# A transformer block with a top-2 mixture of experts: half of the router moved into a pause of attention

## The reference, cut to what matters

```
x: (4, 1024, 128) float32, 16 heads of width 8, 8 experts of width 512, top 2
sa, ca, ga, sb, cb, gb = modulation of each of the four batches
h = layernorm(x) * (1 + ca) + sa
q, k, v = h @ Wq + bq, h @ Wk + bk, h @ Wv + bv
scores = q k^T / sqrt(8), kept where |i - j| <= half   (half at most 60)
x = x + ga * (per-head W_o of softmax(scores) v, then @ Wfc + bfc)
h = layernorm(x) * (1 + cb) + sb
score = relu(h @ rw1 + rb1) @ rw2 + rb2                # (4096, 8)
gate = softmax over the two highest scores of a token, 0 elsewhere
out = sum over e of gate[:, e] * (relu(h @ W1[e] + b1[e]) @ W2[e] + b2[e])
x = x + gb * out
```

## Time and profile before

| | |
|---|---|
| median of 3 runs | 541.64 us (540.28 to 542.08) |
| the profiled execution | 538.34 us, span 536.5 us |
| PE busy | 453.1 us, 84% |
| DVE | 378.4 us, 71% |
| ACT | 349.0 us, 65% |
| POOL | 369.7 us, 69% |

### The profile page before, as it was taken

The page is one execution under the profiler, slowest core; times in us unless marked ns, Lnnn a source line. Parts: engine busy times, 40 slices in busy tenths (PEclk is TensorE's granted clock), DMA queues, the critical chain, the costliest instruction groups (busy, mean ns, idle before and its releaser), DMA issues.

```text
span 536.5 us, 16755 instructions
## 1 busy us (share of the span) xinstructions
PE 453.1 (84%) x5323; PEld 356.0 (66%) x5323; DVE 378.4 (71%) x1026; ACT 349.0 (65%) x1521; POOL 369.7 (69%) x586
## 2 busy tenths in 40 slices
PE   6998888888888888887929996659668999999977
PEld 5565666666666666665504446658447999999977
DVE  6777999999999999999493565735332554555654
ACT  3668999999999999999523552424023787756800
POOL 6975655556688668764447879875888877777640
PEclk9999999999999999999876996969557999999979
DMA  9351000000000400301311121222211222224446
GB/s 236 83 172 46 13 12 13 13 12 13 14 13 12 111 14 14 91 12 44 99 44 34 51 83 51 81 70 79 91 60 61 80 71 82 69 81 137 133 135 194
DMA packets 61519, 36.54 MB, mean 68 GB/s; under 512 B 25806, under 2 KB 57334, under 8 KB 61306
## 3 DMA queue, kind: packets, MB, share of 16 engines
q1 hardware_dynamic: 55834, 25.83, 18.4%
q0 software_dynamic: 4352, 9.45, 5.2%
q10 hardware_dynamic: 1248, 0.20, 0.2%
HBM read 20.56 MB, written 14.88 MB: 66 GB/s over the span
## 4 chain that ended last, share of the span: by engine, by line
PE 35%; DVE 22%; ACT 21%; issue 12%; another core or an unknown queue 5%; POOL 2%; DVEq 2%; ACTq 0%; POOLq 0%
ACT pr L1026 20%; PE pAm L1935 9%; DVE nmax L1093 8%; PE pAm L1485 5%; PE pSpm L1943 5%; PE pScm L1943 4%; PE pScm L1255 2%; DVE oT L947 1%; PE pScm L1500 1%; DVE w1t L1793 1%; DVEq L1552 1%; PE pm L767 1%; DVE stat L1337 1%; PE pSpm L1492 1%
## 5 line engine op out<-in xcount | busy, mean ns | idle before, releaser
L1026 ACT ACTIVATE pr<-pS,nmax 128x136 f32<-128x136 f32 x512 | 185.5, 382 | 13.4 <-DVE nmax L1093 13.2
L1700 ACT ACTIVATE act<-pAm,w1t 128x128 f32<-128x128 f32 x288 | 82.6, 377 | 85.4 <-PE pAm L1935 41.2
L1026 ACT ACTIVATION_READ_ACCUMULATOR pr<-pS,nmax 128x1 f32 x512 | 108.8, 212 | 0.0
L1935 PE MATMUL pAm<-hgT,w1t 128*128 128x128 f32 x576 | 87.2, 293 | 19.3 <-issue 12.8
L1055 PE MATMUL pS<-kT,qbd 64*128 64x136 f32 x1024 | 93.8, 302 | 1.5 <-ACT pr L1026 1.2
L1935 PEld LDWEIGHTS pAm<-hgT,w1t 128*128 128x128 f32 x576 | 77.6, 206 | 24.7 <-issue 20.0
L1647 POOL DMA_INDIRECT y_scr<-ys,si x72 | 73.2, 1016 | 29.7 <-DVE ys L1809 18.0
L1093 DVE TENSOR_REDUCE nmax<-pS 128x4 f32<-128x544 f32 x128 | 87.6, 685 | 2.1 <-PE pS L1059 1.4
L1101 DVE STREAM_TRANSPOSE prT<-pr 128x640 f32<-128x640 f32 x96 | 81.1, 845 | 8.9 <-ACT pr L1026 0.2
L1055 PEld LDWEIGHTS pS<-kT,qbd 64*128 64x128 f32 x1024 | 68.3, 186 | 14.6 <-ACT pr L1026 1.1
L1614 POOL DMA_INDIRECT xs<-h_all,pos_i x64 | 64.0, 999 | 11.3 <-issue 9.6
(11 more groups left out here) (304 smaller groups left out, 716.4 us busy)
## 6 DMA issues: line engine op xcount, KB each, us to landing
hg<-xs SPq DMA_DIRECT2D x72, 72.0 KB
vbd<-v_scr SPq DMA_DIRECT2D x132, 16.0 KB, 1.7
v_scr<-h_all SPq DMA_DIRECT2D x8, 256.0 KB, 2.3
h_all<-y_scr SPq DMA_DIRECT2D x8, 256.0 KB, 3.1
w_all<-y_scr SPq DMA_DIRECT2D x8, 256.0 KB, 5.0
x_all<-in_L_attn_x SPq DMA_DIRECT2D x3, 512.0 KB, 6.1
w_all<-in_L_ffn_W SPq DMA_DIRECT2D x2, 768.0 KB, 4.9
w_all<-in_L_ffn_W SPq DMA_DIRECT2D x3, 512.0 KB, 5.1
```

Source lines behind the costliest of these rows:

```text
L1026: e.activation(pr[:, n, to:to + SPAN], scored(j, gi)[:, lo:lo + SPAN], ACT.Exp, bias=nmax[:, k:k + 1], scale=-1.0, accum_out=rs[u][:, k:k ...
L1700: e.activation(ac(u)[:, k, :], pU[u % W][:, k, :], ACT.Relu, bias=w1t[u // 2 % 4][:, u % 2, FF + D + k:FF + D + k + 1]).then_inc(a_up.sem, 1)
L1935: mm = e.matmul(pU[u % W][:, k, :], w1t[u // 2 % 4][:, u % 2, k * P:(k + 1) * P], hgT[u // 2 % 4][:, u % 2, :], start=True, stop=True)
```

## The change

Attention stops in front of step 20 (FIRST = NT // 2 + 4), and all engines run the router of groups 0 to 3 (G1 = 4) there, in `first_half_*`. Parts 0 and 1 get choices and places in the pause. The choices of part 2 follow behind steps 20 and 21 on DVE, its place in step 23. POOL sends 28 of the first half's 32 dispatches in steps 20 to 31, up to three per step (`send`), without a memset behind them, and the other four after attention. Roots now go by groups of four tiles: on POOL for groups 0 to 2, on DVE for group 3 (in front of the pause), 4 and 5 (a third behind each of steps 23 to 25 and 27 to 29), 6 and 7 (after attention). Behind attention there are four groups. DVE makes both lists of the first half between the scores of groups 4 and 5. In the expert stage the place of part 4 comes at turn 5, and POOL sends two scatters (SOON) ahead of part 4.

```
+            NP1 = 3
+            G1 = NG // 2
+            FIRST = NT // 2 + 4
-            RANKED = 9
+            RANKED = 5
+            SOON = 2
-            BEHIND = {0: 6, 5: 8, 6: 10, 7: 12}
+            BEHIND = {0: 6}
...
+                def send(t, k):
+                    if t < FIRST or sent[0] == NT or k and t % 4 >= 2 and t >= FIRST + 6:
+                        return
+                    if sent[0] == 2 * PARTS[NP1 - 1][0]:
+                        routed(e, NP1 - 1)
+                    dispatch(e, sent[0] // 2, sent[0] % 2)
+                    sent[0] += 1
...
                 def step(i, u, j):
                     maxima(i, u, j, 0)
+                    if 2 * i + u == FIRST:
+                        token_scores(e, G1 - 1)
+                    if 2 * i + u == FIRST + 3:
+                        place(e, NP1 - 1)
...
+                    if t == FIRST - 1:
+                        for part in range(3):
+                            group_refined(e, 3, part)
+                        roots_done(e)
+                    if t in (FIRST, FIRST + 1):
+                        for done in (False, True):
+                            choose(e, NP1 - 1, t - FIRST, done)
+                    for g in (4, 5):
+                        if 0 <= t - (4 * g + 7) < 3:
+                            group_refined(e, g, t - (4 * g + 7))
...
+            def first_half_tensor(e):
+                i, u = (FIRST - 1) // 2, (FIRST - 1) % 2
+                e.wait_ge(d_rw, 64)
+                e.wait_ge(v_k, 3)
+                a_e.wait(e, i, u, 12)
+                turned_rows(e, 0)
+                a_e.wait(e, i, u)
+                for g in range(G1):
+                    if g == 1:
+                        v_o.wait(e, i, u)
+                        a_r.wait(e, i, u)
+                        a_x.wait(e, i, u, back=1)
+                    group_of_router(e, g, 0, G1)
+                partial(e, G1 - 1)
+            def first_half_vector(e):
+                token_scores(e, 0)
+                choose_both(e, 0)
+                token_scores(e, 1)
+                place(e, 0)
+                choose_both(e, 1)
+                token_scores(e, 2)
+                place(e, 1)
+            def first_half_gpsimd(e):
+                group_modulated(e, 2, 3)
+                e.wait_ge(v_gs, 4)
+                for k in range(4):
+                    group_modulated(e, 3, k)
+                routed(e, 0)
+                routed(e, 1)
...
+                for part in range(3):
+                    group_refined(e, 6, part)
                 moment(e, NT - 2)
                 aggregated(e, NT - 4, NT - 1)
                 normalise(e, NI, 0)
+                last_modulated(e, 6)
                 moment(e, NT - 1)
                 aggregated(e, NT - 1, NT)
-                last_refined(e)
-                for g in range(GP, NG):
-                    last_modulated(e, g)
-                token_scores(e, 0)
...
+                for part in range(3):
+                    group_refined(e, 7, part)
+                last_modulated(e, 7)
+                token_scores(e, 4)
                 all_listed(0)
...
                 all_listed(1)
                 token_scores(e, 5)
                 choose_both(e, 3)
                 token_scores(e, 6)
+                place(e, 3)
```

More of the change, by code:

```diff
@@ L190, in build @@
         ohb = [sb(f"ohb{p}", [P, end - first, NE], BF16) for p, (first, end) in enumerate(PARTS)]
-        run = sb("run", [P, NE])
+        run = [sb(f"run{p}", [P, NE]) for p in range(len(PARTS))]
         posg = sb("posg", [P, TPB, NE])
@@ L1631, in route_gpsimd @@
                 residual(e, NI, 0)
-                for k in range(2, 8):
-                    group_modulated(e, 4 + k // 4, k % 4)
                 v_tr.wait(e, NI - 1, 1)
```

216 lines of the change are left out of this document (140 added, 76 removed).

## The result

The changed kernel's median is **546.71 us** (545.84 to 548.53, 4 runs) where the kernel before takes 541.76 (540.28 to 542.08, 4 runs): ratio **1.0101**, 95% interval 1.0069 to 1.0133. Forecast were 533, faster. The profiled execution took 546.40, its span is 544.6, against 538.34 and 536.5.

What follows compares the result with a forecast made beforehand. Attention was taken as bound by DVE and ACT, the experts as slowed by remote waits. +27, +12.6 and +3 in attention left +7 at the first expert product; -15.4 made -8.5: 533 us from 541.64, range 527 to 538.

Steps and rivals of the forecast that it cites:

- the experts' term: Expert stage: fewer dispatches in front of and beside the tiles, results ending at 506.3 instead of 514.8; -15.4 us.
- The pause (+27): In front of step 20: all engines run the router of groups 0 to 3, adding 27 us.
- DVE behind it (+12.6): Steps behind the pause: choices 3.3, place 1.0, token scores 0.3, roots of groups 4 and 5 8 us.
- dispatches (+3): Steps 20 to 31: 28 transfers on POOL between its attention work, 3 us for denominators that come late.
- late denominators: Steps 20 to 31: dispatches delay POOL's own attention work, so denominators come late; counted at 3 us.
- End of attention 297.1: Attention ends at 254.5 + 42.6 = 297.1 us.
- To the first expert product (39.6 us): From the end of attention, with four groups and DVE's lists: first expert product 39.6 us later, at 336.7.
- the slow stretch: Expert stage: returns with part 4's dispatches at 5.9 us per tile for 6 tiles, to about 395 us.
- Rival 1: Expert stage: the slow stretch does not come back, tiles at 1.855 us after tile 5; 510 us, chance 0.23.
- Rival 2: Attention: dispatches hold ACT or PE up, 0.48 us each, and roots cost the high price; 553 us, chance 0.27.

Runs made afterwards that it cites:

- a1: Changed kernel with all 32 dispatches of the first half moved behind attention; 535.3 us, ratio 1.035 to the kernel before on chip 13.
- c_after_again: Unchanged copy of the changed kernel, run on chip 1; 519.5 us, ratio 0.998 to the kernel before.
- d1: Kernel before without the memset behind each POOL transfer, on chip 11; 571.4 us, ratio 1.059 to the kernel before.
- a2: Changed kernel with PE released earlier in step 23, once the place's bank is read; 514.4 us, ratio 0.994 to the kernel before on chip 13.
- h3: Same kernel as a2, measured again on chip 12; 545.7 us, ratio 1.008 to the kernel before.
- b1: Kernel before with only the place of part 4 at turn 5 and two early scatters; 518.3 us, ratio 1.003 to the kernel before on chip 13.

## Why the prediction was wrong, point by point

The sum said -8.5 us and the two spans differ by +8.1. Of these 16.6 us the experts are 9.7, the steps with the pause 6.3 and the start 3.9, less 2.3 and 1.0 that the router and the end gave back. **The step that failed** is the experts' term, -15.4: it let slow issue begin with the dispatches of part 4 and took nothing off the tiles ahead of them. Beside it the two terms for DVE and the dispatches in attention, +12.6 and +3, were too small by 4.9 together.

- **The pause (+27): right.** 213.22 - 178.58 = 34.64 between two oT, against 6.88 for that step before: 27.8. (In five of the 13 traces with the changed attention it is 1.7 us shorter.)
- **DVE behind it (+12.6) and dispatches (+3): 20.5 together.** By the intervals between two oT, each against its own before: the steps with the choices 3.3 and 3.0 where 3.3 was the sum of both; place 4.8 instead of 1.0; the six with roots 8.6 instead of 8.0; another 0.8. a1, without dispatches, gives 15.4 for DVE's part and 5.1 for the dispatches. Of the 28 root instructions, which I had feared most, only two took about 1 us or more (275.07 and 276.39, above). The mistakes: I asked what a dispatch does to POOL's own next work (late denominators), not where it pushes the spread query against DVE; and I priced the place by DVE's time alone, and did not follow PE, which waits for it in front of `project`. The sum also had nothing for the clock: PE's granted clock is 0.90 from 206 to 306 us, where it was 1.00 in the steps of before; what that costs apart from step 23 was not separated.
- **End of attention 297.1: it was 306.4.** (The forecast counts from 254.5, the oT of before is at 253.72.) Of the 10 us (306.44 - 253.72 = 52.7 for 42.6) 5 are the item above and 4 the start, 3.1 of them behind the long sc instruction, which no step of the change explains.
- **To the first expert product (39.6 us): right,** 38.1, with the lists in front of the choices of part 3.
- **The experts (-15.4): -5.7.** This is the term that turned the sign, together with the 6 us that the steps of attention cost more than forecast. Results 10.9 us behind the first product hold where PE issues normally (11.1 on chip 1), but slow issue set in at 354.5, ahead of the first result, and made it 18.0. The place of part 4 was forecast 21.3 us behind the first product and came 30.6 behind it, at 375.2; on chip 1 it took 23.6. Hence the slow stretch, which I had end at 395, ended at 415.4. Its pace of 5.9 us was right, and so were the 1.87 behind it. I took the stretch as tied to part 4 and counted no tiles lost in front of it. This account rests on the traces: no run on a chip with slow issue varied the expert stage's part of the change alone.
- **Rival 1 (no slow stretch, 510)** did not come true in the comparison itself. On two of the four other chips the stretch is missing, but for the kernel before as well, so the change wins nothing by it. What I gave for it, that dispatches, loads and pads might fall together differently, is not what decides it. The Trainium skill ("Runtime: NRT & Kernel Launch", Instruction fetch mechanics), cited there for fetching being hidden, is not contradicted: from 383 to 416 us in the first trace of after the profile has only three packets of kind instruction (q14, 0.02 MB), and those of q8 last 1.13 us on average in that trace and 1.04 in c_after_again, which has no slow issue. d1 shows that POOL's transfers hold the sequencer. By which path, no run shows.
- **Rival 2 (disturbed attention, 553)** was right in its sign and in naming the steps, wrong in its mechanism: there is no remote wait in ACT's exponentials from 206 to 306 us, only 23.2 us for nmax, and a dispatch costs 0.18 us.
- **What I never asked:** how the kernel before would end if nothing held PE up. Then POOL's queue ends last, and what a shorter queue gives is what its later start takes.

No version of the study beats both kernels on every chip: a2 is 0.6% faster than the kernel before on chip 13 and 0.8% slower, under its second name h3, on chip 12.

## What to carry to other kernels

When transfers are moved out of a queue that may bind, count its length from its new start: 32 transfers fewer and 49 us later came to nothing. A stage that waits for "issue" and "remote" should be measured on more than one chip before its time is put into a sum, since the change may be paid for by a stretch that another chip does not have. And between two full engines a small instruction costs what its neighbour on the shared path does at that moment, and what the engine behind it waits for, not its own 0.2 us.

## What the runs showed of the hardware that I had not expected

- The same kernel took 515 to 520 us on chips 1 and 13, 534 on chip 11 and 542 to 543 on chip 12 and in the first comparison. Attention took 197.3 to 197.5 us on all of them; the difference lies in the tiles (185.0, 178.6 and 188.5 us in the three traces of the kernel before, 154.3 in b1 on chip 13) and in the end behind them.
- On chips 11 and 12 PE issues its products singly, 0.72 to 0.77 us apart, while indirect transfers of POOL follow each other without idle time; without the memset of 0.31 us behind each transfer the distance is up to 2.8 us and the kernel before 37 us slower on chip 11.
- A DVE instruction on one element took 4.65 us beside five instructions of POOL in a row in 14 traces, and 0.97 to 0.99 us in six others. In the traces with it the start of the program is 1 to 6 us longer.
